# Attention and expert kernel: square roots for four tiles at once, both copies of the keys on VectorE, output weights, row additions, one exponential and one subtraction at other places

## The reference

```python
def rmsnorm(x, gamma):
    norm = jnp.sqrt(jnp.sum(x * x, axis=-1, keepdims=True)) * x.shape[-1] ** (-0.5)
    return x / jnp.maximum(norm, RMS_EPS) * gamma
...
qn = rmsnorm(q, qn_g) * SCALE
kn = rmsnorm(k, kn_g)
attn = jnp.einsum('bhid,bhjd->bhij', qn, kn)
...
attn = jax.nn.softmax(attn, axis=-1)
out = jnp.einsum('bhij,bhjd->bhid', attn, v)
```

## Time and profile before

| what | value |
| --- | --- |
| median of three executions | 985.15 us |
| lowest and highest of them | 976.21 and 987.36 us |
| the profiled execution's own time | 974.24 us |
| its span, first to last instruction | 972.4 us |
| busy: PE, DVE, ACT, POOL | 802.3, 560.4, 400.9, 353.3 us |
| mean granted TensorE clock | 0.92 |

### The profile page before, as it was taken

How to read it: one execution, slowest core, us unless ns; L and a number is a source line. 1 busy time by engine, 2 the same in 40 slices (tenths; PEclk the granted TensorE clock), 3 DMA queues, 4 the chain that set the end, 5 groups by cost and what they waited for, 6 DMA issues and landing times.

```text
span 972.4 us, 12802 instructions
## 1 busy us (share of the span) xinstructions
PE 802.3 (83%) x4832; PEld 637.7 (66%) x4832; DVE 560.4 (58%) x1132; ACT 400.9 (41%) x719; POOL 353.3 (36%) x296
## 2 busy tenths in 40 slices
PE   2659988989999999978999587774029999999998
PEld 2546554655655455767799487774019888998897
DVE  5766686566676663463334676754944555655532
ACT  2324543453454344631712433323006554665563
POOL 5523112310310112253521343122242786666763
PEclk9959999999999999997999998976558999999999
DMA  6000000000000100100020101111210542245422
GB/s 172 1 0 1 1 1 1 1 1 1 1 1 1 45 2 1 44 1 3 0 83 31 57 1 44 44 44 49 92 39 6 137 131 76 72 131 136 124 32 26
DMA packets 21371, 39.70 MB, mean 41 GB/s; under 512 B 4489, under 2 KB 16893, under 8 KB 19005
## 3 DMA queue, kind: packets, MB, share of 16 engines
q1 hardware_dynamic: 14653, 30.44, 9.3%
q0 software_dynamic: 6656, 8.43, 4.9%
HBM read 30.32 MB, written 8.40 MB: 40 GB/s over the span
## 4 chain that ended last, share of the span: by engine, by line
PE 48%; DVE 23%; POOL 11%; issue 10%; ACT 6%; DMA 1%; SPq 0%; ACTq 0%; DVEq 0%; POOLq 0%
PE ps L409 14%; PE ps L548 9%; PE ps L648 5%; PE ps L988 5%; DVE mx L1151 4%; POOL out_dram L2344 3%; PE ps L512 3%; POOL gt L2221 3%; PE ps L565 2%; PE ps L566 2%; POOL wh L2339 2%; DVE qkn L1110 2%; PE ps L489 1%; DVE oh L1593 1%; DVE rep L1525 1%
## 5 line engine op out<-in xcount | busy, mean ns | idle before, releaser
L548 PE MATMUL ps<-PT,VA 128*65 128x512 f32 (+1 forms) x288 | 148.0, 596 | 0.2 <-ACT PT L1759 0.2
L988 PE MATMUL ps<-wh,he 128*128 128x256 f32 (+1 forms) x960 | 127.3, 288 | 0.0
L988 PEld LDWEIGHTS ps<-wh,he 128*128 128x128 f32 (+1 forms) x960 | 112.2, 172 | 6.5
L1759 ACT ACTIVATE PT<-ps 128x512 f32<-128x512 f32 x128 | 76.0, 594 | 67.5 <-PE ps L566 67.0
L1151 DVE TENSOR_REDUCE mx<-ps 128x1 f32<-128x1104 f32 x64 | 83.5, 1304 | 34.8 <-PE ps L512 34.6
L409 PE MATMUL ps<-GT,wh 128*128 128x258 f32 x768 | 96.4, 288 | 1.1 <-DVE GT L1614 1.1
L409 PEld LDWEIGHTS ps<-GT,wh 128*128 128x128 f32 x768 | 95.5, 194 | 1.7 <-issue 1.5
L2080 POOL TENSOR_TENSOR ssq<-ssq,half 128x4 f32<-128x4 f32 x32 | 32.4, 1012 | 126.9 <-DVE ssq L1092 126.6
L2071 POOL TENSOR_TENSOR rs<-rs,half 128x4 f32<-128x4 f32 (+1 forms) x18 | 17.4, 968 | 162.8 <-DVE rs L1024 162.6
L1627 DVE TENSOR_TENSOR he<-het,he 128x516 fp32r<-128x516 f32 x64 | 44.8, 700 | 54.8 <-ACT he L1653 54.3
L2344 POOL DMA_INDIRECT out_dram<-ye,idx x40 | 66.5, 1663 | 22.6 <-ACT ye L1653 15.4
(11 more groups left out here) (251 smaller groups left out, 1591.5 us busy)
## 6 DMA issues: line engine op xcount, KB each, us to landing
wr<-in_w1e_dram SPq DMA_DIRECT2D x8, 1024.0 KB, 4.8
wr<-in_w2e_dram SPq DMA_DIRECT2D x8, 1024.0 KB, 7.7
x<-in_x_dram SPq DMA_DIRECT2D x4, 512.0 KB, 7.1
w<-in_w_dram SPq DMA_DIRECT2D x2, 1024.0 KB, 4.8
y_dram<-yr SPq DMA_DIRECT2D x4, 512.0 KB, 3.0
out_dram<-x SPq DMA_DIRECT2D x4, 512.0 KB, 4.1
b2e<-in_b2e_dram SPq DMA_DIRECT2D x8, 128.0 KB, 7.3
gt<-y_dram,idx POOLq DMA_INDIRECT x40, 2.8
```

Source lines behind the costliest of these rows:

```text
L548: pe.matmul(bank[6 + hf][0:65, :], VA[b][0:K, kt, h, :], PT[u % 4][0:K, :], start=kt == 0, stop=kt == 8).then_inc(p_pv, 1)
L988: op = pe.matmul(bank[bk][0:M, 0:256], he[j][:, m, c0:c0 + M], w2h[i][:, 256 * m:256 * m + 256], start=n == 0, stop=n == 23)
L1759: a.activation(PT[u % 4][0:K, :], bank[4 + u % 2][0:K, :], ACT.Exp, bias=0.0 if K == 128 else mcol[:, b:b + 1]).then_inc(a_exp, 1)
```

## The change

- Roots: the four sums of a group are taken one by one (now `v_ssq`), but scaled once as 128x16, and POOL takes one root of 128x16 for each group (two for each proj where there were eight).
- Copies: DVE writes both copies of `qkn` (128x2048) and of `kcn` in one instruction each; POOL's halves are gone.
- Output weights: `wo_in` has its own memory, the ACT copy of `wo` moves into unit 1 of attention 0, and POOL's subtraction behind all roots of proj(0, 0).
- Row additions: the first two add_rows now stand on POOL behind the first root of proj(0, 1).
- head(0, 1) runs beside attention 0; MAX_AT and SIDE_RATE for head 0 follow.
- Layer 1: ACT does the exponential of tile n+2 behind the copy of tile n.
- Search: POOL's 128x2048 subtractions are cut into 128x512 pieces, one behind each of the first eight rounds.

```diff
-MAX_AT = (4, 6, 7, 9, 10, 12, 13, 15)
-SIDE_RATE = (1.0, 1.4, 1.4, 1.0, 1.0, 1.0, 1.0, 1.0)
+MAX_AT = (5, 6, 8, 9, 10, 12, 13, 15)
+SIDE_RATE = (1.4, 1.4, 1.4, 1.0, 1.0, 1.0, 1.0, 1.0)
...
 # tensor_program, vector_program and scalar_program alike
-            h_ = head(0, 1, lambda n: 6 + n % 2)
             for qt in range(4):
                 max_tile(0, qt)
-                next(h_, None)
             max_row(0, 0)
-            drain(h_)
-            beside = [spaced(proj(0, 1, side, False), head(0, 2, side)), ...
+            beside = [spaced(head(0, 1, side), proj(0, 1, side, False), head(0, 2, side)), ...
...
 # vector_program, proj
-                        step(v.tensor_reduce(ssq[:, 0, 4 * t:4 * t + 4], sq[:, :].rearrange("p (h d) -> p h d", h=4), AX.X, ALU.add))
-                        settle()
-                        v.tensor_scalar(ssq[:, 1, 4 * t:4 * t + 4], ssq[:, 0, 4 * t:4 * t + 4], 1.0 / DH, 1e-16,
-                                        ALU.mult, ALU.max).then_inc(v_ms, 1)
+                        v.tensor_reduce(ssq[:, 0, 4 * t:4 * t + 4], sq[:, :].rearrange("p (h d) -> p h d", h=4), AX.X,
+                                        ALU.add).then_inc(v_ssq, 1)
+                        if t == 3:
+                            v.wait_ge(v_ssq, 8 * P + i + 1)
+                            v.tensor_scalar(ssq[:, 1, :], ssq[:, 0, :], 1.0 / DH, 1e-16, ALU.mult, ALU.max).then_inc(v_ms, 1)
...
-                    v.tensor_tensor(qkn[:, 4 * gi:4 * gi + 4, :, :, :].rearrange("p t h a d -> p (t h) a d")[:, :, 0, :],
-                                    qkr[:, :, :].rearrange("p t (h d) -> p (t h) d", d=DH),
-                                    ssq[:, 2, 0:16].unsqueeze(2).to_broadcast([128, 16, DH]), ALU.mult).then_inc(v_qkn, 1)
+                    v.tensor_tensor(qkn[:, 4 * gi:4 * gi + 4, :, :, :].rearrange("p t h a d -> p (t h) a d"),
+                                    qkr[:, :, :].rearrange("p t (h d) -> p (t h) d", d=DH).unsqueeze(2).to_broadcast([128, 16, 2, DH]),
+                                    ssq[:, 2, :].unsqueeze(2).unsqueeze(3).to_broadcast([128, 16, 2, DH]), ALU.mult).then_inc(v_qkn, 1)
...
 # scalar_program, attention and attention1
+                    if hi == 0 and u == 1:
+                        a.wait_ge(g_wo, 1)
+                        a.wait_ge(d_w, 144)
+                        copy(wo[0], wo_in).then_inc(a_whi, 1)
...
-                    if n + 2 < NT:
-                        exps(n + 2)
                     yield
                     a.wait_ge(p_pT, n + 1)
                     if n >= 2:
                         a.wait_ge(p_pv, 144 + n - 1)
                     copy(PT1[n % 2][0][:, :, :], src).then_inc(a_pT, 1)
+                    if n + 2 < NT:
+                        exps(n + 2)
                     yield
...
 # gpsimd_program
+            def root_q(P, gi):
+                g_.wait_ge(v_ms, 2 * P + gi + 1)
+                g_.tensor_tensor(ssq[:, 2, :], ssq[:, 1, :], half[:, :], ALU.pow).then_inc(g_rq, 1)
...
             for j, w_ in enumerate((wh1, wh2[0])):
-                g_.wait_ge(a_wh, j + 1)
-                g_.tensor_tensor(w_[1][:, :], wr[j][:, :], f(w_[0][:, :]), ALU.subtract).then_inc(g_wh, 1)
+                for i in range(4):
+                    c = slice(512 * i, 512 * i + 512)
+                    g_.wait_ge(v_rnd, 4 * j + i + 1)
+                    if i == 0:
+                        g_.wait_ge(a_wh, j + 1)
+                    op = g_.tensor_tensor(w_[1][:, c], wr[j][:, c], f(w_[0][:, c]), ALU.subtract)
+                op.then_inc(g_wh, 1)
```

More of the change, by code:

```diff
@@ L315, in build @@
         v_xt = sem("v_xt")
+        v_ssq = sem("v_ssq")
         v_ms = sem("v_ms")
@@ L340, in build @@
         v_sub = sem("v_sub")
+        v_rnd = sem("v_rnd")
         v_rec = sem("v_rec")
@@ L833, in tensor_program @@
             drain(c_, p_, h_)
-            h_ = head(0, 1, lambda n: 6 + n % 2)
             for qt in range(4):
                 max_tile(0, qt)
-                next(h_, None)
             max_row(0, 0)
-            drain(h_)
-            beside = [spaced(proj(0, 1, side, False), head(0, 2, side)), spaced(head(0, 3, side), ln(1, side), ctx(1, side)),
+            beside = [spaced(head(0, 1, side), proj(0, 1, side, False), head(0, 2, side)), spaced(head(0, 3, side), ln(1, side), ctx(1, side)),
                       spaced(proj(1, 0, side, True), head(1, 0, side)), spaced(head(1, 1, side)),
@@ L1464, in vector_program @@
             drain(c_, p_, h_)
-            h_ = head(0, 1, lambda n: 6 + n % 2)
             for qt in range(4):
                 max_tile(0, qt)
-                next(h_, None)
-            drain(h_)
             made["unit"] = 0
             made["ctx_bank"] = 3
-            beside = [spaced(proj(0, 1, side, False), head(0, 2, side)), spaced(head(0, 3, side), ln(1), ctx(1)),
+            beside = [spaced(head(0, 1, side), proj(0, 1, side, False), head(0, 2, side)), spaced(head(0, 3, side), ln(1), ctx(1)),
                       spaced(proj(1, 0, side, True), head(1, 0, side)), spaced(head(1, 1, side)),
@@ L1536, in vector_program @@
                 settle()
-                step(v.tensor_tensor(C_, Q_ if n < 9 else P_, E_, ALU.bitwise_or))
-                settle()
+                v.tensor_tensor(C_, Q_ if n < 9 else P_, E_, ALU.bitwise_or).then_inc(v_rnd, 1)
+                v.wait_ge(v_rnd, n + 1)
             def bte(ap):
@@ L1750, in ot @@
                         a.wait_ge(p_wo, 8 * (hi - 1) + 4 * hf + 4)
+                    else:
+                        a.wait_ge(g_wlo, 3)
                     copy(OT[0][:, qc], bank[6 + hf][0:65, :]).then_inc(a_ot, 1)
@@ L1927, in scalar_program @@
                 next(first)
-            a.wait_ge(g_wo, 1)
             a.wait_ge(d_w, 144)
-            copy(wo[0], wo_in).then_inc(a_whi, 1)
             p_, h_, c_ = proj(0, 0, lambda n: 2 + n % 4, True), head(0, 0, lambda n: 6 + n % 2), ctx(0, 0)
@@ L1944, in scalar_program @@
             drain(c_, p_, h_)
-            h_ = head(0, 1, lambda n: 6 + n % 2)
-            for qt in range(4):
-                next(h_, None)
             max_row(0, 0)
-            drain(h_)
-            beside = [spaced(proj(0, 1, side, False), head(0, 2, side)), spaced(head(0, 3, side), ln(1, side), ctx(1, 3)),
+            beside = [spaced(head(0, 1, side), proj(0, 1, side, False), head(0, 2, side)), spaced(head(0, 3, side), ln(1, side), ctx(1, 3)),
                       spaced(proj(1, 0, side, True), head(1, 0, side)), spaced(head(1, 1, side)),
@@ L2246, in gpsimd_program @@
             g_.wait_ge(g_wo, 1)
+            factors(("ctx", 0), 0, 1, SC)
+            root_q(0, 0)
+            root_c(0)
+            root_q(0, 1)
             g_.wait_ge(a_whi, 3)
             g_.tensor_tensor(wo[1], wo_in, f(wo[0]), ALU.subtract).then_inc(g_wlo, 1)
-            root_q(0, 0)
-            root_q(0, 1)
-            factors(("ctx", 0), 0, 1, SC)
-            root_q(0, 2)
-            root_c(0)
-            root_q(0, 3)
-            twice_kc(0)
-            scale_qk(0, 0)
-            for t in range(4):
-                root_q(0, 4 + t)
-            scale_qk(0, 1)
+            root_q(1, 0)
             g_.wait_ge(d_rows, 48)
@@ L2271, in gpsimd_program @@
             root_c(1)
-            twice_kc(1)
-            proj(2)
-            proj(3)
+            for P in (2, 3):
+                root_q(P, 0)
+                root_q(P, 1)
             lnf(0)
```

55 lines of the change are left out of this document (12 added, 43 removed).

## The result

The changed kernel took 987.01 us (median of 20 executions, 982.05 to 990.93) against 978.86 us (975.13 to 987.36, 20 executions): a ratio of 1.0066, 95% interval 1.004 to 1.0092. It is slower by 0.7%, where no change was forecast. That 987.01 lies only 2 us from the forecast's 985 on the median is luck: those 985 rest on the first three executions of the kernel before, whose median of 985.15 lies 6.3 us above the median of all 20. The profiled execution took 982.05 us against 974.24, +7.81.

The account below looks back on a forecast made before the run. PE was taken to bound attention 0, chains of waits on DVE, POOL and ACT other stretches. 974.24 + 0.45 + 12.35 + 3.6 - 10.1 - 6.4 = 974.1 us, no change; 985 on the median, range 968 to 996.

Parts of the forecast that it names:

- The wide root: POOL's 128x16 root takes 2.7 us, now waited for in full, 1.7 more for each of eight groups.
- Cheap root: Rival, chance 0.14: POOL's 128x16 root costs only 1.0 us, 10.4 us off in all, 963.7.
- The double write: DVE's write of both copies of qkn takes 2.2 us alone, so the copy costs nothing and leaves POOL free.
- The start: Stretch before attention 0: first group +2.4, context's layer-norm factor -0.5, second group -1.45, together +0.45 us.
- Attention 0: Transposes +1.0, POOL's subtraction +0.5, two PE pauses +8.85, lower clock +2.0: +12.35 us.
- Attention 2 and 4: Four groups, scaling to end of qkn 5.0 us instead of 4.1: +0.9 each, +3.6 us, or 0 if PE's queue hides it.
- Layer 1: Copy ahead of exponential: plain tiles gain 0.9 us, 14 tiles together -10.1, between -5 and -15.
- The search: POOL's subtractions in 128x512 pieces no longer hold DVE: -6.4 us, between -5.5 and -6.9.
- On the shared pair: DVE and POOL: whichever starts first has the pair for its whole instruction; the new place costs one add_row.
- Clock lost in attention 0: Rival, chance 0.2: PE stays at 1.2 GHz after two 6 us pauses, granted clock under 0.75 for over 15 us: 984.1.
- Stalls taken up: Rival, chance 0.18: DVE precedes add_row (-2.2), clock holds (-2.0), layer 1 gives 7.6 us more: 962.3.
- the ACT reorder does nothing: Rival, chance 0.08: in layer 1 ACT's copy always waits for PE; +8 us, 982.1.

Follow-up runs that it names:

- the small roots: The changed kernel with DVE's scaling and POOL's root taken as 128x4 for each tile again: 972.6 us, ratio 0.9928 to the kernel before.

## Why the prediction was wrong

The picture held and the balance didn't. The terms came to -0.1, and the stretches that they speak of measured 1.32 + 12.89 + 6.95 - 6.39 - 6.81 = +8.0. Of the difference of 8.1, layer 1 is 3.7, attention 2 and 4 are 3.35, the start is 0.9, attention 0 is 0.5 and the search -0.4. So two steps failed: the sum gave layer 1 nearly its full gain in 14 tiles, and it counted a clock loss behind pauses for attention 0 alone.

- **The wide root**: 2.7 forecast, 2.90 measured. *Cheap root* falls. The extra 0.2 stands in each of eight groups. That the root is waited for in full is what the small roots show: 15.3 us in four stretches.
- **The double write**: 2.2 forecast, 2.29; beside a row addition 4.4 forecast, 4.41.
- **The start**: +2.1 counted from the fourth sum, for +0.45 (+0.95 without the context's factor, which lies ahead of it). The first group's write ended at 42.73 instead of 40.65; counted from the sum that is 2.8 later, for 2.4. In the second group the scaling came 0.65 us later behind the first write than before (DVE waited 1.22 us for ACT's KB there, for 0.27), which was not in the sum, and from its end to the end of the write it took 5.3 us for 5.0. Taking head(0, 1) out gave 0.6, for nothing. The context's root behind the wide one was in the sum, with its kcn and value copy at 1.8; with small roots it costs 1.9 at the first write.
- **Attention 0**: +12.89 for +12.35, with idle times of 6.27 (forecast 6.35) and 3.13 (5.65, too long: PE had 5.1 us queued behind its last projection, not 2.0). Idle time grew by 7.2, where 8.85 were forecast, and PE's busy time by 5.7, where about 3 were; 16 transposes at 0.60 for four are at most 2.4 of them, and at least 3 us are the clock, where 2 were forecast. The first pause was read rightly; that the total fits so well is luck, as two errors cancel.
- **Attention 2 and 4, the first step that failed**: "+0.9 each, +3.6". Attention 2 gave 1.73, attention 4 gave 5.22. From the scaling's end to the write's end each group took 4.13 to 4.15 us before and 5.30 to 5.32 after, +1.2 for +0.9, so the path was read rightly and its size nearly. In the second group of attention 4 the maximum stands behind the write in both kernels, and PE waits for it. Timelines of DVE and PE before, then after, then two windows of after:

```profile
271.89 2.31 DVE L1110 TENSOR_TENSOR qkn<-qkr,ssq 128x1024 f32<-128x1024 f32 x1
...
275.47 0.63 PE L409 MATMUL ps<-wo,OT 65*128 65x258 f32 x3 [1.33 <-DVE mx L1151]
```

```profile
288.12 0.18 DVE L1090 TENSOR_SCALAR ssq<-ssq 128x16 f32<-128x16 f32 x1
291.31 2.29 DVE L1107 TENSOR_TENSOR qkn<-qkr,ssq 128x2048 f32<-128x2048 f32 x1 [1.10 <-POOL ssq L2072]
293.52 1.30 DVE L1148 TENSOR_REDUCE mx<-ps 128x1 f32<-128x1104 f32 x1
...
294.88 1.02 PE L410 MATMUL ps<-wo,OT 65*128 65x258 f32 x3 [2.50 <-DVE mx L1148]
297.40 1.91 PE L548 MATMUL ps<-PT,VA 128*65 128x512 f32 x2
```

```profile
289.00:294.00 5.00, 3.13 (x10) 1.21 (x8) 3.87 (x5) 1.24 (x3) 2.28 (x1) 1.00 0.00 0
294.00:299.00 5.00, 4.12 (x12) 2.80 (x12) 2.15 (x4) 1.19 (x2) 0.00 (x0) 0.57 0.00 0
```

  The pause grew from 1.33 to 2.50 us, and behind it the granted clock is 0.57 and, from 299 to 304, 0.74: values products of 1.02 take 1.91. Of the head's +5.2, 2.4 are idle time, as the two groups' 1.2 say, and 2.9 are PE's busy time at the lower clock. No clock term was in the sum for this head. With small roots this pause is 1.31 us, no fall follows, and the head takes 41.92. The size of the clock's part varies: in four other profiles with the same pause the head took 45.85 to 47.25 us.
- **Layer 1, the other step that was mis-sized**: "A plain tile gains 0.9", -10.1 in all; measured -6.39. The wait fell from 26.3 to 12.1 us, and DVE waits for scores instead. The prediction gave every one of 14 tiles nearly its full gain. Counted from one subtraction of scores to the next, five periods gained 0.8 to 0.9 and one 1.2, three of the plain ones 0.2 to 0.6, and four gained nothing or lost up to 0.4; the end of the stretch, with two tiles priced at 0, gained 1.8. The first period lost 1.46 (5.23 for 3.77 us), but it took 5.23 in the kernel with the search edit alone too, so that this part is chance, and without it the gain is 7.85, where the ACT edit alone gave 7.8. Timeline of PE, the same 12 score products behind a pause of the same length, in after and in the kernel with the ACT edit alone:

```profile
577.79 3.20 PE L410 MATMUL ps<-WK,xt 128*128 128x308 f32 x12 [2.62 <-DVE Pb L1346]
```

```profile
558.59 1.95 PE L409 MATMUL ps<-WK,xt 128*128 128x308 f32 x12 [2.62 <-DVE Pb L1349]
```

  After 2.62 us without work PE ran at the lower clock in one execution and at the full one in the other, in which plain tiles took 3.82 and 3.96 us, better than the 4.1 of the forecast. In nine profiles with this edit the stretch took 107.2 to 108.6 us, in three 111.2 to 112.7, with granted clocks of 0.83 to 0.85 there against 0.86 to 0.88. The bound of the plain tiles was read right, that of the others was not, and PE's clock was not priced here either.
- **The search**: -6.81 for -6.4. All pieces of 1.27 us started within 0.1 us of a round and held nothing.
- **On the shared pair**: DVE waited for one addition and went ahead of the other, which then took its turn (6.71 us for the two against 4.65 where DVE left them alone). The wait was 4.41 - 2.29 = 2.12 us. By the rule of the Trainium skill, "SBUF — State Buffer", section "SBUF: two separate sides", the one that starts first has the pair for its whole instruction, so the wait is one addition's; here the traces agree. The row at 37.38 does not fit: DVE began first there, and still its half ended 1.09 us behind POOL's, as in six of the other seven groups (1.08), in all of which POOL began first. No run takes this up.
- *Clock lost in attention 0* was half right: the granted clock was 0.52 and then 0.80 in the ten us from 100 on, and 0.52 and 0.79 from 117 on, so not under 0.75 for over 15 us at once, but the same effect came again in attention 4, where no rival looked. Its price of 12 us for 25 us of PE's work at half the clock was too low in itself: at 1.91 for 1.02 it would be some 22, an estimate. *Stalls taken up* and *the ACT reorder does nothing* fall.

Stretches that no edit touches moved as well: -3.7 from attention 7 to layer 1 and +2.0 from the last round to the end. The first took 176.0 to 182.7 us over all fourteen profiles and the second 267.7 to 270.3, so both are chance; in the first PE's busy time differs by 3.8, and the clock between 441 and 451 us was 0.56 before, with nothing so low after. Over all executions the difference is 0.66%, so the profiles' +7.8 is a fair size all the same.

What stays open: why the clock falls behind one pause of PE and not behind another of the same length, as in the two rows of layer 1. Attention 1 has a third case: its +1.08 is PE's busy time (40.96 for 39.77 us) at a granted clock of 0.96 for 1.00, behind a pause of 1.62 us that was 1.59 before and cost nothing. No run varied a pause alone.

## What to carry to other kernels

Making an instruction wider on an engine that has time to spare, to save its fixed cost, moves the cost onto the path if the narrow ones were hidden and the last one alone was waited for. Ask for each queue what stands behind the wait that grows, ACT's as well as DVE's. Where PE is the bound, price a pause as the pause plus PE's work at the lower clock that may follow it, wherever the pause is and not only in the head under study. A gain in one wait that recurs in 14 tiles is not 14 times the gain of the plain one. A long GpSimd operation that stands right behind the result VectorE waits for takes the shared pair first; one wait that holds it back until VectorE's write is done made the start 4.1 us shorter here.

## What the runs showed of the hardware

- GpSimd's power takes 0.56, 1.01 and 2.90 us for 1, 4 and 16 numbers for each partition: 0.15 to 0.16 us for each further number, 32 roots of 128x4 32.2 us and eight of 128x16 23.2 us.
- VectorE's 128x2048 write with broadcast takes 2.29 us. When GpSimd wrote half of it, GpSimd's half took 1.9 us, and VectorE's ended 1.08 us behind it, 2.98 us for both, in all six groups beyond the start: the times are those of two halves one after the other, and sharing the work took longer than VectorE alone.
- A VectorE instruction on 64x80 numbers (0.24 us) took 2.30 us where a GpSimd addition had begun just before it.
- Behind a pause of PE of 2.62 us the granted clock fell to the lower level in one execution and not in another: the same 12 products took 3.20 and 1.95 us.
